# Four chained attention layers on one core: new order strings and a new bank table for the same beats

## The reference

```python
def attention(xq, xkv, wq, wk, wv, wo, mask):        # A0 ... A5, each with its own weights, biases and mask
    q, k, v = heads(xq @ wq), heads(xkv @ wk), heads(xkv @ wv)
    s = q @ k.T / 4                                  # A3: s = s * fside, then -inf where its mask says
    return merge(softmax(where(mask, s, -inf)) @ v) @ wo
x = norm(x + A0(x, x)); x = norm(x + A1(x, ctx)); x = norm(x + relu(x @ w1 + b1) @ w2 + b2)   # layer 0: A0, A1, F0
x = norm(x + A2(x, ctx))                                                                      # layer 1
x = norm(x + A3(x, ctx))                                                                      # layer 2
x = x + A4(norm(x), ctx); x = x + A5(norm(x), norm(x)); x = x + gelu(norm(x) @ w1 + b1) @ w2 + b2   # layer 3
```

## Time and profile before

| what | before |
|---|---|
| median of 3 runs (lowest, highest) | 1228.22 us (1225.85, 1228.24) |
| profiled execution | 1226.54 us |
| its span, first to last instruction | 1224.7 us |
| TensorE busy | 1182.9 us, 97% |
| VectorE busy | 783.5 us, 64% |
| ScalarE busy | 484.0 us, 40% |
| GpSimd busy | 207.1 us, 17% |

### The profile page before, as it was taken

How to read it: one execution, slowest core, us unless ns; L and a number is a source line. 1 busy time by engine, 2 the same in 40 slices (tenths; PEclk the granted TensorE clock), 3 DMA queues, 4 the chain that set the end, 5 groups by cost and what they waited for, 6 DMA issues and landing times.

```text
span 1224.7 us, 35043 instructions
## 1 busy us (share of the span) xinstructions
PE 1182.9 (97%) x14292; PEld 956.4 (78%) x14292; DVE 783.5 (64%) x2123; ACT 484.0 (40%) x1126; POOL 207.1 (17%) x319
## 2 busy tenths in 40 slices
PE   5999999999999999999999999999999999999987
PEld 4877888877778888787788687888778778877866
DVE  4556577786986556555876856665785676467641
ACT  1343333322344363353344254434334435343533
POOL 0022122211111012111211121022022012112110
PEclk9999999998999999999999999999999999999998
DMA  7700001011202000001110100100011001001000
GB/s 248 295 2 2 2 3 44 2 44 44 88 2 71 6 14 6 6 9 49 45 56 6 44 13 16 35 18 13 6 44 56 6 17 45 1 7 44 11 6 10
DMA packets 22940, 43.98 MB, mean 36 GB/s; under 512 B 6528, under 2 KB 16896, under 8 KB 19712
## 3 DMA queue, kind: packets, MB, share of 16 engines
q1 hardware_dynamic: 21824, 40.30, 9.2%
q10 hardware_dynamic: 960, 1.44, 0.3%
HBM read 39.63 MB, written 2.10 MB: 34 GB/s over the span
## 4 chain that ended last, share of the span: by engine, by line
PE 76%; DVE 11%; issue 9%; POOL 2%; SPq 1%; DMA 0%; ACT 0%; POOLq 0%; DVEq 0%; ACTq 0%
PE bank L662 21%; PE bank L655 19%; PE bank L752 6%; PE bank L648 6%; PE bank L704 6%; PE bank L729 6%; DVE neg_max L1002 4%; PE bank L724 3%; PE bank L696 3%; PE bank L740 2%; DVE weight L1112 2%; PE bank L718 2%; DVE weight L1106 1%; PE bank L765 1%; POOL root L606 1%
## 5 line engine op out<-in xcount | busy, mean ns | idle before, releaser
L1002 DVE TENSOR_REDUCE neg_max<-bank 128x4 f32<-128x512 f32 x320 | 201.6, 682 | 51.4 <-PE bank L704 51.3
L606 POOL TENSOR_TENSOR root<-var_eps,halves 128x1 f32<-128x1 f32 x128 | 73.7, 577 | 832.4 <-DVE var_eps L1054 832.2
L875 ACT ACTIVATE exps_t<-bank 128x512 f32<-128x512 f32 x320 | 169.6, 609 | 90.9 <-PE bank L740 90.5
L662 PE MATMUL bank<-x_t,weights_A 128*128 128x128 f32 x1024 | 136.7, 282 | 2.8 <-ACT x_t L857 2.6
L662 PEld LDWEIGHTS bank<-x_t,weights_A 128*128 128x128 f32 x1024 | 125.7, 195 | 11.7 <-ACT x_t L857 4.9
L662 PE MATMUL bank<-x_t,weights_F 128*128 128x128 f32 x1024 | 125.8, 280 | 1.0 <-ACT x_t L857 0.9
L662 PEld LDWEIGHTS bank<-x_t,weights_F 128*128 128x128 f32 x1024 | 121.2, 195 | 4.6 <-ACT x_t L857 1.7
L655 PE MATMUL bank<-weights_F,exps_t 128*128 128x256 f32 x512 | 120.5, 382 | 0.0
L704 PE MATMUL bank<-k_eo,q_t 32*128 32x256 f32 x1536 | 111.0, 399 | 0.0
L752 PE MATMUL bank<-exps_t,v_one 128*32 128x128 f32 x3072 | 105.7, 276 | 2.1 <-ACT exps_t L875 0.8
L857 ACT COPY x_t<-bank 128x256 f32<-128x256 f32 x128 | 46.7, 381 | 153.2 <-PE bank L648 153.1
(11 more groups left out here) (104 smaller groups left out, 1734.0 us busy)
## 6 DMA issues: line engine op xcount, KB each, us to landing
weight<-in_fside SPq DMA_DIRECT2D x16, 1024.0 KB, 4.9
weights_A<-in_weights_A SPq DMA_DIRECT2D x4, 1028.0 KB, 18.2
weights_F<-in_weights_F SPq DMA_DIRECT2D x2, 2054.0 KB, 16.9
drop_raw<-in_drop SPq DMA_DIRECT2D x16, 256.0 KB, 5.3
x_hat<-in_x SPq DMA_DIRECT2D x16, 128.0 KB, 2.1
out<-x_sum SPq DMA_DIRECT2D x16, 128.0 KB, 1.7
ctx_t<-in_ctx_t SPq DMA_DIRECT2D x13, 128.0 KB, 4.9
rows_A<-in_rows_A SPq DMA_DIRECT2D x3, 512.0 KB, 19.0
```

The source lines that it names most:

```text
L606: nc.gpsimd.tensor_tensor(root[x][:], var_eps[x][:], halves[:, e:e + 1], ALU.pow).then_inc(done["root"], 1)
L662: mm = nc.tensor.matmul(dst[:, 128 * f:128 * f + 128], w[:, c, 128 * f:128 * f + 128], tokens_t[:, c, :], start=(c == 0), stop=(c == KC - 1))
L875: nc.scalar.activation(dst, score_bank(x, "ST", s, j)[:], ACT.Exp, scale=DH ** -0.5).then_inc(done["exp"], 1)
L1002: nc.vector.tensor_reduce(neg_max[x][:, j, :], heads, AX_X, ALU.max, negate=True).then_inc(done["max"], 1)
```

## The change

The generators, the instructions of every beat and their waits' form stay. New are the five order strings and the three tables of places. Both versions of every string hold each item's digit equally often. The new TENSOR string differs from the old in 1561 of 1607 places. Read through `tensor_lane`, the last beats of TENSOR are, before: 14 Y1, 15 nT (A5), 15 O, 15 xT (F1), 15 H0, 15 H1, 15 Y0, 15 Y1; and after: 14 Y1, 15 nT (A5), 13 xT (F1), 15 O, 13 H0, 13 H1, 13 Y0, 15 xT (F1), 13 Y1, 15 H0, 15 H1, 15 Y0, 15 Y1. The longest strings other than TENSOR are cut here.

```diff
--- before.py
+++ after.py
@@ -184,79 +184,79 @@
 
 
 TENSOR = """
-12345112100100230011101340000101010100201000212202201301222222300001002033100023104033333111102113001113202042130432
-12514404204422224441301154532232112403550330404321033330002055514314324555555032305200431111054440414411140533521214
-25434134122522551342222003515555554002312440000002545203330352333324554114110052335031111031144444144413543405002252
-40000222220432215015450202155555533413330533311505411113120253150013324444144422204105022220000123411302423040455352
-53312211421533335551113040051201415065322663521466442222466666464646613251416536363364176776774532677772537777772342
-66764746633636357667562765555447652777667777776767532835887637887688888868888787866666866678787663854388867558878888
-67878777767678388688747438587639799444454998696699996969696998889898888789869864894555965569998959597799987967977776
-89799997674574988649887498888866796999969696979864a96aa986aa987657a7aaaa7a7a7a7aa986a9a96875aa667a78a999999aaa9a9a9a
-aaa9688a9785a795a668888aa8aa8785a976666a9675a5b9bba6ababaabbbbbabababbbaab6ba99a86797b7a6baba779999778b98766bbb796cb
-bbbccbccbaaabcaccccacacacaccbaca8cba8bbcbcbca7988cb8bcccbcccc8888ccbbcbbcbbbbbba79caccccbab99c7caab7bacaa7bcaa7dcddc
-cddccccca9dcb9ca8dddddcddddbdcbbdcbbbbbbd8adcdbb8a9ada99999dddbd9dcddddcdccdcccccbcd8bddddcbbbc8d8bbbbadcbacdb98cbd8
-edeeddb9cadddeedddce9dceeeececececeedae9bed9da9ecbaedcaaaea9b9feffbcaffdaeeefbffffefefefeffeefdfeddedddddfdcfeadcfee
-ffeffeffffffdeafecefdcdeafaffffacefeefbfbeeeebbbdeefbfeffeffffffddefdbefeddddbccfdcfbdccccdceeeeeeeeeedbcdebfedbbbdd
-eceffffffeffffddfedcfddeeceeeeddfcfedfedcecfffedffeeffdefedfdeefeddfeeeeffeffeeffefeffffeefefffffff
+13425112100200440203300001121121222402211110002230011204004440013013303124120000253500003333444410023032013511103400
+00043555250345021111555532212134515033134532222333020133111145230012321000041020522021111200453442324030254441111441
+41504131432222224225541510442203432002315555000025500235333504333300433415311130504424355354441114410244245211045121
+45004200202023051202105205052005555551553333050513333332402300300010101121113443144024410224441514102222404211202011
+12064556624256111136156666323321666653555333426655631653424246365163133666611175444422226775766646767757763777727763
+72474626667674337364647526777266777733336773674557342273287887856666555487888876653488887887683863543865398997865444
+4979767979777797789545999988978966796694588886666898798785466898889686545995984848799995555998564988984a56aa9788886a
+a889aaaa999875797896aaaa7777966aa878a9989a795999966669655a6975a9698a75b8abb9889baaba7bb9bb6766aaaabbbb88887baba86ba6
+ba999987b9999a8baaaa89966b6a9666a89a6b86bbbaabbbbabba6b9aaaa787baa968a7777babbbba67a6b67ab76b6c7ccbbbb7c88c7abbbb888
+8cc9ccbbab8aab89799b8b7ccccaaa9a999bcc8aa8c8c797a78cac897777b97bbb8bbca7bb88ac9bb79b9b78888accc89ccccacc8b9cbc877c99
+8cccc87c7dcdd888e9ddeecaad99a99aeceddde9eeecddddeeeeaaceeddecdeda9ccccbcecdedac9acbed999dedddac99faffcfeeddddddfedff
+cfdfaeeeeffffeffedaededcfdfedeefeefadcecdecefccccacdceeceefdeedddcadeedddaddeedcfbfbfdecffffbbaaaabbdffdefabfdbaebea
+cfffffddbcddbbfaddddccafddfeccccdadffcffacbffffffceafbfecdeedfcfcbbfbebeeebbbcbeeceefbfffbffffdffecccefbdcccefbbeeeb
+fbeceeeddfcefceddddedcffdfdeffffeefdcefefddcfdedffeecfeeeedfcedefdcefddddefdeedffffdefefdfdddfdffff
 """
 VECTOR = """
-01234511211010101230000013400222202000012033300001012313010022111101024031132222202041044343403151201400000555352253
-33353112421204434051311431114444504333202000251545000000005001201400222545550523234141341235155023313121131311001114
...
+01423511211110001424000020223322012444443333031000000111000020410225325110011312000555513533004002222325033331321445
+40000103112331145125033513224424111100414122005200240222555545214120000010104043040203103051224434022323133131550021
...
 """
 SCALAR = """
-12345010110111000001001220222212230000012303333031111021300123412222404444241311420355300400333213025555425530543111
...
+13425000001100211112222210021204444014343331332000000342301311110400355555504215222235133334523011130002010252201111
...
 """
 POOL = """
-00112000200301131224143302005523411435425024003531511440022255113332424004113535566442277666776353578876868887799868
-464699997776698889aa7755aa999aa886b6ababbccbba979aa7ccccbbccddaabbb88dddcdccbb99ddeeccaafefeeedddffffeeffdbdbeeeccff
-feeddffeeff
+00112200030030441111532252320001443134224500503355441110052252333110042424611633555676427462677337786865579978844866
+8699995858aa6967977babaa88a8999bba66abb77bb88ccaa9a977bbbc8c8cceded9a9cacddeefdfedecccddefefbafbafdddccffeeebbfffeec
+dcdffeeddff
 """
 SYNC = """
-0010122123334455450123456666077718882999378aaa94abbb5ccc6bddd7cdeee8fff9eafbcdef
+001321044331422555012345666067771888299937aaa48bbb95accc6bcdddeee78fff9deafbcedf
 """
 
 EXP_PLACES = """
-21222211222112122211211222111112112000100001200212112222212211112201010012012210110110111011110000111010101100101111
-111102221122
+21002102220000201110000120200000220201120000012012112222111202202202201222222222112000000222021001011111001222202022
+201111222111
 """
 OUT_PLACES = """
-100001100101001000001110100101010001001111110101101001101110100011011100011100111000001000001111
+100010011011011000110000000001001111001110110011100101111111100100000001111101101011111011000000
 """
 
 PLACES = """
-76574475012357415216074123560472137421302356743232347610546217603542716343140276350271436720752071412713560413253535
-23746105273163014605171624031714134356203630714507126301707361645203716343031760752437024165741230647276426477426715
...
+76546645012354612357041236501037426501357403612573460173524607126312121547016352524637102514034761253717517540637140
+14634627501436217313137121540672137541457420631574203720231654702316412016753461626262162617176053247165304353237416
...
 """
```

More of the change, by code:

```diff
@@ L205 @@
[L205 to L209, removed]
@@ new lines @@
+40000103112331145125033513224424111100414122005200240222555545214120000010104043040203103051224434022323133131550021
+11113115151010450330444400343103222222222322525425004400011445421151514515530323213030330303530353511311515025232200
+25000303442444443434434342342122023411001405514515555525545411111212542454066624266663633135362222224446455314616613
+36535666656335561777577776746555575276633673733732424426676777747646666767736774474444332838888888877665787886686553
+95899777867878899998966667666666769645657897767999889788558655569999594448866866698887887879957777777979897674aaa666
@@ new lines @@
+6aaaa8a86a9995578589899999a78888878988a8a96a888898a6699aaaa6a7975b7bb7897bbbbba9999b9696979997979aba7787966b6aba6ba8
+696baa88a9988bbbb8ba99aaaa6a89b99bba8888b8baab696aaa6bb7abaaba7a7aa7bbbb6cbaccaaaaba7accccc79999c9bb8abbb88b7877777b
+bbcbab8bac8cb9cbbbbabcab88888a8a97a9bcccc9cabb77979bbbaaaaca8bbcc9999c9c898cb8ccc7dcdd8eddddedeccccceeeeed9eedceedad
+ebdcbcbedbb99aac9eeeddddedecacd9faffcfffffddecccdcfdcadceccfeccccceeeffdfddeefaaeaaaadeceeefefffecddcddfdedcccccddee
+fddcdffdeebafedfdbddfdeddcdcddcdcdcdabafbfafdbbfddffeffefeededeecdfdeedeeefefccacbbbfbfbbfedcfcffffffffffefefbfccece
@@ L215 @@
+ccefebcbeddddffdbeeeeefeffffbfcefffffedecceddcdeefeefefdfdeeedddddffdfffffefceeeddddfefffdf
 """
 SCALAR = """
[L217 to L220 removed]
@@ new lines @@
+14342444303145412222242555514043200005023533330431531111054443445412452220214000002510255055553333351320300000111113
+41444204222214024020111265411555516666663333316526365342226244441316167666524677777767772466674333633752777726736666
+7555532787765488888838786833546844495479779777999989889887696666486978888965499998555544958698888a5978a9aaaaa9879777
+6a766a686a999995965a65798ba98888aaaabb7bbbb6abb8ba99999b79a8aa6666a6986bbbbbabaaaa6b9a77778a7bbba66b67c7bbbbb88c88ab
+8cccccbaaaa89999b9cac98c7a7777c97bbbbb8a7b888c89b78ccccca8bc7c978cc8cd8e9999dadaaa9cedddedeeeedecceccaded9cedacb99de
@@ L225 @@
+9ddddacfeedeefdfffffeffdeddfceeefdecccccaeceeefdeddddedaaaadcffffbbbbefadbfbaefffdbcddddfadccccacdafffffcfefcdeeeefb
+bbbbebefbfffffeccccfdcbbebeeeefceddddcedfdffffefdcfcfeeeeecdeefdddddeffffedeffdddfff
 """
 POOL = """
[L227 to L229 removed]
+00112200030030441111532252320001443134224500503355441110052252333110042424611633555676427462677337786865579978844866
@@ new lines @@
+36231305743157417603245176041472350647273714503147256127265256043166256720431567230324023742013425253267014236236714
+36450273651460300432675432104672521717617305426713206731420540246502473463274350173304517302643737171650326754165047
+13647052170635072414325460314075630721017154206713424517046351246703075307412654712304651273045614565214765015712612
+67340512673431205462156437026464156347102461026075432106257140256256523573530300376214530756546713205647132360451212
+31276034512451570660670241307423256712531704261737137573735371262507314625037403127652407310650246765327530147360342
@@ new lines @@
+51734645032145754654646450675362727442710536274627054261307542621431463207420304312567310426360357143040265704326272
```

(8 more changed lines are left out.)

26 lines of the change are left out of this document (removed).

## The result

| | before | after |
|---|---|---|
| median (lowest, highest) | 1228.17 us (1225.85, 1228.24) | 1180.23 us (1180.10, 1182.37) |
| ratio, 95% interval | 1 | 0.9618 [0.9602, 0.9635] |
| span of the profiled execution | 1224.7 us | 1178.4 us |
| TensorE busy | 1182.9 us | 1143.4 us |

The account below looks back on a forecast made before the run. TensorE, busy 1182.9 of 1224.7 us, was taken as the bound, with time lost to its changes of form. 1226.5 - 23 (forms) - 7 (tail) - 7 (middle) = 1189.5, rounded down to 1188 us; range 1176 to 1202, held at 0.67.

Parts of the forecast that it names:

- TensorE's forms: TensorE's beats use the whole array, 32 rows or 32 columns; fewer changes between these forms save 23.0 us.
- exits: Leaving 32 rows or 32 columns for whole-array work on TensorE: 285 before, 199 after, 8.6 us saved at 0.10 each.
- entries: Whole-array work followed by a small form on TensorE: 173 before, 87 after, 7.7 us saved at 0.09 each.
- maskless S or ST behind 32-row work: S or ST without an opening mask product, directly behind 32-row work: 5 before, 28 after, 2.1 us saved.
- changes between 32 rows and 32 columns: TensorE switching between its two small forms: 28 before, 53 after, 2.5 us lost at 0.10 each.
- The tail: Item 15's bare last chain gets filled, removing gaps and half clock: 7 us saved, bounds 2 and 9.
- The middle: Visible TensorE waiting between 24 and 1186 us, 18.7 us: 7 credited; bounds 15 credited or 12 more waiting.
- Rival (a): Form changes go but most returns as 8 to 20 us of new waits: 1202 to 1224 us; chance 0.15.
- TensorE's busy time: Sign in the profile after: TensorE's busy time falls by some 25 us, to 1158.
- Idle time of the middle: Sign in the profile after: TensorE idle for 10 to 15 us over 24 to 1155 us.
- The start: TensorE's wait for loads of x and first products from 16.59 us: forecast unchanged.
- Rival (c): Too little time for the longest handover, O to next xT; slower, 1234 us at 0.4 us mean miss; chance 0.04.

Follow-up runs that it names:

- e1: The changed kernel with TENSOR beats moved so that TensorE changes form about as often as before, all else kept: 1215.96 us.
- e2: The changed kernel with item 13's last stage moved back ahead of item 15's chain, ScalarE and VectorE orders matched: 1188.34 us.
- e10: The changed kernel with S and ST swapped at its 13 places of ST, S, shift, banks kept: 1196.69 us.
- e11: e8 with S and ST swapped at its 13 places of S, ST, shift, banks kept: 1190.51 us.
- e8: Orders and place tables annealed on from the changed kernel with form prices and trace durations, first fold kept out of the start: 1161.65 us.
- e3: The changed kernel, all orders kept, with a bank table by a plain rule (bank read longest ago): 1181.10 us.

## Why the prediction was right, and where it was off

**TensorE's forms: 23.0 forecast, 27.2 found.** The mechanism holds and its size nearly: e1 takes it back by itself and loses 25.7 us of usual distance. One of my readings was wrong, and several counts with it, and the description of the beats ahead of the prediction is wrong in the same place: S of A3 does not open with a mask product over the whole array, its sixteen score products stand alone. Counted rightly, exits fall from 280 to 188 (92, not 86), of them into products from 179 to 108 as forecast, entries from 184 to 92 (92, not 86), maskless S or ST behind 32-row work rise from 8 to 37 (29, not 23), and changes between 32 rows and 32 columns from 30 to 55. With the prediction's own prices that is 9.2 + 7.1 + 8.3 + 2.6 - 2.5 = 24.7 us. The other 2.5 us are prices rounded down to 0.10 and 0.09 where the shortest fifths give about 0.11 and 0.095, and a term that I left out: a transpose right behind an exit also takes 0.05 us longer, and of these there are 14 fewer (63 to 49). For the unpriced change between 32 rows and 32 columns the traces give 0.11 to 0.13 us, near the 0.10 that I took. The durations themselves stay: in the trace after, four L655 instructions take 0.86 us behind whole-array work (73.08 to 73.94) and 0.97 behind a shift (378.38 to 379.35).

The Trainium skill, "TensorEngine Tiling (Array Packing)", Key Properties, has a change of tiling mode drain TensorE, without a figure. Counting all changes alike (335 after, 497 in e1) at 0.10 us would give e1 16.2 us; its distances show 25.7, so here a count of changes alone is too low by over a third, and entry and the product behind the exit have to be priced too.

**The tail: 7 forecast, 11.2 found.** This is the term that I sized too low. I had 6.6 us of gaps and 2.2 of half clock and then took 7 of the 8.8; all of it went. And I overlooked two things. O of items 14 and 15 each waits 0.7 us for o_t behind nT, which the two rows of O in the earlier trace rows show in part (0.55 us of idle time). And besides the stretch at 1210 us the trace of before has another behind the other 2.56 us gap, windows view and timeline of before:

```profile
1193.00:1197.00 4.00, 3.78 (x38) 2.29 (x39) 0.49 (x2) 0.27 (x1) 1.11 (x2) 0.57 0.00 0
```
```profile
1193.28 1.91 PE L724 MATMUL bank<-idb,sxs_bias 128*128 128x512 bf16 x4
1195.12 1.82 PE L729 MATMUL bank<-q_t,k_eo 32*128 32x128 f32 x32
```

A5's mask product of item 15 takes 1.84 us there (1193.28 to 1195.12) instead of 0.96, and that ST as a whole 1.5 us more than usual. With 6.6, 1.4, 2.3 and 1.5 us, and 0.3 ahead of H of item 14, the 12.1 us of the table are complete; 0.9 us are waited after the change. With both gaps gone, no half clock is left in the tail (granted 1.00 over 1130 to 1178 us). e2 confirms the mechanism for item 15's chain alone.

**The middle: 7 forecast, 7.8 found, for half a reason.** The pairs that I counted did get more room: waits in or behind S fall from 7.2 to 2.5 us, behind mT from 5.5 to 0.9, behind ST from 7.2 to 2.0, behind oT from 3.3 to 1.5. With nT and O some 18 us go, more than twice what I credited. But behind shift 7.1 us come, and behind xT 2.8 (1.2 to 4.0), which I had not named; e10 and e11 show what the first of them is, for 13 places. So the sum is right by luck: two larger numbers, of which I had priced neither, happen to differ by about my 7. Rival (a), new waits as the price of fewer form changes, is thus true in kind and wrong in size: the waits that came are smaller than those that went. And 18.7 us was not all the waiting that there was: 46.0 us were, and e8 got 17.5 of them back.

**What I had said would show it.** TensorE's busy time fell by 39.5 us, not 25: 27.2 are the forms, 3.8 the half clock of the tail, and 7.5 are waits of the middle too short to show, which stand in busy rows as well (7.8 fell, 0.3 of it in idle time). The three come to 38.5. Idle time of the middle was to be 10 to 15 us and is 18.4, a sign that did not come, though the waits did fall: where waits of under half a microsecond are partly hidden in the rows, idle time is no measure of them. Groups of PV of x96 stand six times in the new order, once in the old. No gap of 2.8 us stands in the tail.

**Costed at nothing.** The start is the same to 0.1 us in the table (7.0 and 11.3). The found bank table is worth nothing over the plain rule in the new orders (e3). Eight ScalarE table loads fewer save that engine 9.4 us of busy time, and it is busy for 40% of the span; no experiment took this by itself. Rival (c), the long handover missed, did not come about: of TensorE's waits from 24 to 1132 us in the trace after, the profile puts one down to x_hat, 0.3 us.

What stays open: e10 and e11 settle 13 of the 22 waits behind shift; the others (among them ST behind ST, and S, ST, shift with an exp as the releaser, 0.74 us) I only read in the trace. e8 is one order from one search; its profit is not shown for another. Nor is it shown how much of e8's shorter middle comes from them and how much from the other beats.

## What to carry to other kernels

When one engine is 97% busy, look at what the same instruction takes behind different neighbours: here grouping TensorE's work by form was worth 27 us of 1225 without removing an instruction, more than the 18.7 us of idle time that the profile showed in the middle. Measure waits by distances between starts, not by idle time, and price each regrouping against what it fills up (here all eight banks); try it both ways, since the cheaper wait depends on the surroundings. And look at the last 50 us by themselves: a bare chain costs its gaps and then the slower clock behind them.

## What the runs showed of the hardware that I had not expected

- Half clock comes behind a gap of 2.56 us in TensorE's work each time the tail had one (before at 1193 and 1210 us, e2 at 1173.9 us), and behind the long folds of one-column products although TensorE is busy for all of those stretches (after: 7.00 of 7 us at 0.53). Only taking the gaps away ended the first kind; the second stayed in every kernel. One stretch is of neither kind: in e10 the granted clock is 0.57 over 712 to 716 us, behind an S of A1 with waits of 0.69 and 0.24 us in its midst.
- The two sides of a form change are priced apart: about 0.11 us to leave 32 rows or 32 columns, about 0.10 more for the float32 product behind it, 0.05 to 0.06 for a float32 transpose in that place and 0.01 for the bf16 one (mT), and 0.095 to enter.
- Which of two beats that write different banks for different items (S and ST) comes first matters a good deal, and by the place and not by a rule: swapping them cost 7.0 us of waits over 13 places in e10 and 20.7 over 13 in e11, in opposite directions.
